# One convolution block goes from GpSimd to ScalarE and VectorE, and one input projection goes between two transposes

## The reference, cut to what matters

```python
zxbcdt = x @ in_proj_w.T
z = zxbcdt[..., :D_INNER]
xBC = zxbcdt[..., D_INNER:D_INNER + CONV_DIM]       # 384 channels
xp = jnp.pad(xBC, ((0, 0), (D_CONV - 1, 0), (0, 0)))
conv = conv_b
for k in range(D_CONV):                             # 4 taps
    conv = conv + xp[:, k:k + L, :] * conv_w[:, k]
xBC = jax.nn.silu(conv)
dt = jax.nn.softplus(zxbcdt[..., D_INNER + CONV_DIM:] + dt_bias)
```

## Time and profile before

| | |
|---|---|
| median of 3 runs | 872.43 us (872.13, 872.43, 874.5) |
| the profiled execution's own time | 876.48 us |
| its span | 874.8 us, granted clock 0.981 |
| PE busy | 796.5 us (91%) |
| VectorE busy | 605.7 us (69%) |
| ScalarE busy | 496.4 us (57%) |
| GpSimd busy | 365.4 us (42%) |
| GpSimd L1655, the sums of the convolution | 48 x 1302 ns = 62.5 us |
| GpSimd L1652, the products | 48 x 757 ns = 36.3 us |

### The profile page before, as it was taken

One profiled execution on the slowest core, in us unless ns is written; L12 is line 12 of the kernel. 1 busy time (PEld: TensorE's weight loads), 2 busy tenths in 40 slices (PEclk: granted clock), 3 DMA queues, 4 the chain that ended last, 5 costly groups with the idle time before them and its releaser, 6 DMA issues. The chain is left out here.

```text
span 874.8 us, 18230 instructions
## 1 busy us (share of the span) xinstructions
PE 796.5 (91%) x5472; PEld 492.2 (56%) x5472; DVE 605.7 (69%) x1443; ACT 496.4 (57%) x952; POOL 365.4 (42%) x656
## 2 busy tenths in 40 slices
PE   2789999999999999999899999999999998999897
PEld 1554564755647556565647555475555656475555
DVE  2576469784787757786687847877587866878534
ACT  2325774467743675547744678436854577446652
POOL 5633627054541627227280454516272272804500
PEclk9897999999999998999999999999999999999999
DMA  4000000000000100000000000000000000000000
GB/s 163 1 3 18 14 1 1 9 16 25 0 1 6 33 5 0 7 12 25 0 0 7 13 24 0 1 7 26 11 0 7 12 26 0 0 7 13 24 1 13
DMA packets 15145, 11.73 MB, mean 13 GB/s; under 512 B 1040, under 2 KB 13968, under 8 KB 14992
## 3 DMA queue, kind: packets, MB, share of 16 engines
q1 hardware_dynamic: 15120, 11.43, 4.3%
HBM read 7.76 MB, written 2.10 MB: 11 GB/s over the span
## 5 line engine op out<-in xcount | busy, mean ns | idle before, releaser
L1097 ACT ACTIVATE sb_pr<-S 128x768 f32<-128x768 f32 (+1 forms) x192 | 165.8, 890 | 130.8 <-PE S L444 130.8
L1194 DVE TENSOR_REDUCE sb_mx<-S 128x2 f32<-128x256 f32 (+3 forms) x256 | 197.7, 816 | 41.7 <-PE S L444 41.1
L1715 POOL TENSOR_SCALAR_AFFINE_SELECT sb_pr<-sb_pr 128x256 f32<-128x256 f32 (+1 forms) x192 | 98.9, 517 | 292.7 <-ACT sb_pr L1097 289.4
L444 PE MATMUL R<-sb_pr,sb_va 128*32 128x512 f32 (+3 forms) x1024 | 89.7, 445 | 0.0
L444 PE MATMUL S<-sb_kT,sb_qT 32*128 32x256 f32 (+3 forms) x512 | 56.8, 386 | 19.7 <-DVE sb_mx L1194 15.8
L444 PE MATMUL R<-sb_W,sb_pr 128*128 128x96 f32 (+1 forms) x512 | 69.5, 276 | 0.0
L444 PE MATMUL R<-sb_xfT,sb_W 128*128 128x512 f32 x144 | 69.2, 602 | 0.0
L444 PEld LDWEIGHTS S<-sb_kT,sb_qT 32*128 32x128 f32 x512 | 27.8, 184 | 73.0 <-DVE sb_mx L1194 65.2
L444 PEld LDWEIGHTS R<-sb_W,sb_pr 128*128 128x128 f32 x512 | 63.5, 192 | 3.8 <-issue 3.5
L1655 POOL TENSOR_TENSOR sb_cv<-sb_cv,sb_cm 128x512 f32<-128x512 f32 x48 | 62.5, 1302 | 4.0
L444 PE MATMUL S<-sb_qT,sb_kT 32*128 32x256 f32 (+3 forms) x512 | 56.8, 387 | 5.6 <-ACT sb_pr L1097 4.8
(11 more groups left out here) (216 smaller groups left out, 1711.2 us busy)
## 6 DMA issues: line engine op xcount, KB each, us to landing
sb_xin<-x SPq DMA_DIRECT2D x9, 256.0 KB, 2.7
sb_W<-weights SPq DMA_DIRECT2D x1, 2290.0 KB, 9.9
sb_qT<-sb_mT SPq DMA_DIRECT2D x128, 4.0 KB
sb_xres<-x SPq DMA_DIRECT2D x8, 256.0 KB, 2.8
out<-sb_xres SPq DMA_DIRECT2D x7, 256.0 KB, 2.3
sb_cT<-sb_xact SPq DMA_DIRECT2D x8, 128.0 KB, 2.3
sb_W<-weights SPq DMA_DIRECT2D x1, 514.0 KB, 4.6
sb_cst<-consts SPq DMA_DIRECT2D x1, 328.0 KB, 3.0
```

What stands on the lines that cost most here:

```text
L444: return pe.matmul(o, lhsT, rhs, start=start, stop=stop, skip_group_check=True)
L1097: act.activation(pr[:, e % 4, :, 0:n], S[pair_of_exp(e)][:, :, 0:n], ACT.Exp).then_inc(p_sb, 1)
L1194: o = dve.tensor_reduce(mx[:, n // P - 1, g, heads[0]:heads[1] + 1], found[:, :, at_col:at_col + n], AX.X, ALU.max, negate=True)
L1715: pool.affine_select(out=keep, in_=keep, compare_op=ALU.is_ge, fill=0.0, base=0, pattern=pattern, channel_multiplier=-1)\
```

## The change

It does three things. GpSimd keeps block 2 of the convolution alone (seven instructions less). Block 1 goes to ScalarE, which now makes the beginnings of blocks 0 and 1 ahead of the `qT` copies, and to VectorE, whose table now has six taps. On PE `project_x(r, 2)` moves from ahead of `project_z(r, 0)` to behind the transposes of `x1n`.

```diff
-TAP_AT = {2: (0, 2), 4: (0, 1), 6: (0, 0)}
+TAP_AT = {0: (0, 2), 2: (0, 1), 4: (0, 0), 6: (1, 2), 8: (1, 1), 10: (1, 0)}
...
                 if head:
                     project_x(r, 1)
-                    project_x(r, 2)
                     project_z(r, 0)
                     project_z(r, 1)
...
                 if head:
+                    project_x(r, 2)
                     project_z(r, 2)
...
                     evac_z(r, 3)
 
+                    for n in range(2):
+                        tap = V_CONVW + TAPS * n + TAPS - 1
+                        act.wait_ge(xc_sb, at(xc_sb, r, n + 1))
+                        act.wait_ge(conv_sb, at(conv_sb, r, 0))
+                        act.activation(cv[:, n], xc[:, n, TAPS - 1:TAPS - 1 + L], ACT.Identity,
+                                       bias=vec[:, V_CONVB + n:V_CONVB + n + 1],
+                                       scale=vec[:, tap:tap + 1]).then_inc(conv_act, 1)
                     act.wait_ge(e_ps, at(e_ps, r, 0))
...
-                    act.wait_ge(xc_sb, at(xc_sb, r, 1))
-                    act.wait_ge(conv_sb, at(conv_sb, r, 0))
-                    act.activation(cv[:, 0], xc[:, 0, TAPS - 1:TAPS - 1 + L], ACT.Identity,
-                                   bias=vec[:, V_CONVB:V_CONVB + 1],
-                                   scale=vec[:, V_CONVW + TAPS - 1:V_CONVW + TAPS]).then_inc(conv_act, 1)
...
-                    act.wait_ge(conv_dve, at(conv_dve, r, TAPS - 1))
-                    act.wait_ge(conv_pool, at(conv_pool, r, 2 * (2 * TAPS - 1)))
+                    act.wait_ge(conv_dve, at(conv_dve, r, 2 * (TAPS - 1)))
+                    act.wait_ge(conv_pool, at(conv_pool, r, 2 * TAPS - 1))
...
                 if k == TAPS - 2:
-                    dve.wait_ge(conv_act, at(conv_act, r, 1))
+                    dve.wait_ge(conv_act, at(conv_act, r, n + 1))
                 else:
-                    dve.wait_ge(conv_dve, at(conv_dve, r, 2 - k))
+                    dve.wait_ge(conv_dve, at(conv_dve, r, (TAPS - 1) * n + 2 - k))
...
-                    for n in (1, 2):
-                        base = at(conv_pool, r, (n - 1) * (2 * TAPS - 1))
+                    n = 2
```

More of the change, by code:

```diff
@@ L301, in build @@
         act_up = signal("act_up", 17)
-        conv_act = signal("conv_act", 1)
+        conv_act = signal("conv_act", 2)
         conv_sb = signal("conv_sb", 1)
@@ L331, in build @@
         kT_sb = signal("kT_sb", G)
-        conv_dve = signal("conv_dve", TAPS - 1)
+        conv_dve = signal("conv_dve", 2 * (TAPS - 1))
         mx_sb = signal("mx_sb", G * UNITS)
@@ L354, in build @@
         qw_sb = signal("qw_sb", 1)
-        conv_pool = signal("conv_pool", 2 * (2 * TAPS - 1))
+        conv_pool = signal("conv_pool", 2 * TAPS - 1)
         spa_sb = signal("spa_sb", 3)
@@ L1642, in stage_b @@
                     pool.sem_inc(pool_passed, 1)
-                    for n in (1, 2):
-                        base = at(conv_pool, r, (n - 1) * (2 * TAPS - 1))
[L1645 to L1655, removed]
+                    n = 2
+                    ts(cv[:, n], xc[:, n, 3:3 + L], vec[:, V_CONVW + 4 * n + 3:V_CONVW + 4 * n + 4],
+                       vec[:, V_CONVB + n:V_CONVB + n + 1], ALU.mult, ALU.add).then_inc(conv_pool, 1)
+                    for i, k in enumerate((2, 1, 0)):
+                        tap = V_CONVW + 4 * n + k
+                        if i:
+                            pool.wait_ge(conv_pool, at(conv_pool, r, 2 * i + 1))
+                            pool.sem_inc(pool_passed, 1)
+                        ts(cm[:], xc[:, n, k:k + L], vec[:, tap:tap + 1], 0.0, ALU.mult,
+                           ALU.add).then_inc(conv_pool, 1)
+                        pool.wait_ge(conv_pool, at(conv_pool, r, 2 * i + 2))
+                        tt(cv[:, n], cv[:, n], cm[:], ALU.add).then_inc(conv_pool, 1)
                     time_steps(r)
```

## The result

The changed kernel takes 866.6 us in the median of 20 runs (one, at 1860.09 us, lies far outside and is left out of every comparison; the other 19 lie at 862.86 to 874.31, with a median of 866.52) against 874.77 us for the kernel before (20 runs, 872.05 to 878.32): a ratio of 0.9912, 95% interval 0.9896 to 0.9929. Forecast were 869.5 us and a range of 865.5 to 876.0. The profiled execution took 864.34 us, its span is 862.6 us and its granted clock 0.993, against 876.48, 874.8 and 0.981.

A forecast was written before the change was run, and what follows sets the result against it. PE was taken as busy nearly all the time, slowed by clock falls and waits for VectorE. The profiled 876.48 us less 5.9 (clock) less 1.1 (seven rounds) gave 869.5 us, range 865.5 to 876.0, own range 868.0 to 871.0.

The forecast's parts named there:

- The clock: PE's tokqk transposes: with idle time moved away from just ahead, all three loop falls go, saving 5.9 us.
- The prologue: Rival: the clock also holds in the prologue's 32 transposes, 2.9 us less, 866.6 us; chance 0.08.
- ScalarE's delay: Two beginnings ahead of the first qT copy make PE wait about 0.5 us a round within the transposes.
- The rival that it is hidden: ScalarE's copies overlap, so PE never waits for qT: 4.6 us less in all, 866.0 us; chance 0.12.
- The lead of a round: Net gain of a loop round from VectorE's work: 0.15 us, 1.1 us over seven rounds.
- PE's group of g = 1: PE's wait of 0.88 us at its second score group goes; after the 0.5 us delay, PE is about 0.35 early.
- the tap behind m = 8: VectorE's added 0.66 us tap in 0.45 us of idle time: 0.2 too much, lead falls from 0.35 to 0.15.
- Behind m = 10: VectorE's added 0.66 us tap against 0.72 us back from the step freed of rs: lead stays 0.15 to 0.2.
- The meeting with `rs`: Rival: GpSimd's rs holds up VectorE's gate steps, 4.9 us more over seven rounds; 875.5 or 877.3 us; chance 0.20.
- The step behind m = 0: VectorE's added tap beside GpSimd's block may take 1.16 us, yet fits its idle time to within 0.1.
- The frame: Terms count from the profiled 876.48 us; the runs' median, 872.43, is 4.05 lower; without falls both meet near 870.6.

The follow-up runs named there:

- e1: Kernel before with only project_x(r, 2) moved behind the x1n transposes, convolution as before: ratio 0.9953 to the kernel before.
- e2: Changed kernel with project_x(r, 2) put back ahead of project_z(r, 0), so the convolution change alone: ratio 0.9958 to the kernel before.
- e8: Kernel before with four unread matmuls in PE's idle time ahead of the xf transposes, in the loop: ratio 0.9931 to the kernel before.
- e4: Changed kernel with four unread matmuls where the projection left, ahead of the x1n transposes, in the loop: ratio 0.9884 to the kernel before.
- e6: Changed kernel with the alterations of e3 and e4, plus six unread matmuls in the prologue: ratio 0.9811 to the kernel before.
- e7: e6 with block 1's last tap behind m = 12 instead of m = 10: ratio 0.9808 to the kernel before.
- e5: Changed kernel with GpSimd still doing its seven block 1 instructions, into an unread spare tile: ratio 0.9994 to the kernel before.
- e3: Changed kernel with ScalarE's two beginnings behind the fourth qT copy instead of ahead of the copies: ratio 0.9851 to the kernel before.

## Why the prediction was right, and what it mis-sized

- *The size and the luck in it.* The forecast of 869.5 is right to 0.3%, but not by its sum. From profile to profile it had 7.0 us (5.9 clock, 1.1 rounds) and the two profiles differ by 12.1; the range of its own, 868.0 to 871.0, missed 866.6. Two errors hid each other: the sum was too small by 2.1 us in the rounds and 4.1 in prologue and start, and too bold in that every fall would go, which the median run does not show.
- *The clock.* Right in its mechanism, which e1 against e2 and e8 show: where PE idles counts, and not only how much. Too bold in its size: that all falls go. One was left in this execution, for 4.9 us instead of 5.9, and six of the 19 runs, at 871.7 to 874.3 us with a mean granted clock of 0.978 to 0.980, must have several and the slow prologue, as e2's profile has; of the rest, 0.988 to 0.996, all but one lie under 867. The 0.93 us of idle time that only moved is what is left: filled (e4, e6, e7), the times near 872 us are gone. Why one round falls and the next, with the same times on PE ahead of it, does not, stays open. The three falls of the old profile cost 1.65 + 2.95 + 1.65 = 6.25 us by the lengths of their rounds, 0.35 more than the 5.9 of the sum.
- *The prologue.* I gave its clock 0.08 as a rival; it came true in this profile, and in those of e1 and e5, for 2.9 us. In e3 and e4 it did not, with the same stream on PE. The three profiles without the moved projection (before, e2, e8) all have slow transposes there. So the move may help, but does not decide; what does stays open. Filled, they took 3.7 us in both profiles (e6, e7).
- *ScalarE's delay.* 0.5 us a round forecast, 0.55 measured, all of it paid in an undisturbed round (e3). The rival that it is hidden is refuted there; it is true of the rounds in which the clock falls.
- *VectorE and GpSimd.* The lead of a round was 0.15 us in my sum and is 0.46. At PE's group of g = 1 I had 0.35 and it was 0.41 (442.58 - 416.81 = 25.77 against 26.18). The term that was mis-sized is the lead behind that group, in three steps. I took PE's 0.35 for VectorE's lead at the reduction of m = 8; but that reduction waits for nothing (454.08, 443.55) and follows VectorE's own work, which was 0.52 ahead at m = 6, so it came 0.49 ahead. With the tap behind m = 8 I let the lead fall by 0.2, and it fell by 0.1, to 0.38. Behind m = 10, where freed and added time were to cancel, it rose by 0.1. Seven rounds of 0.3 are 2.2 us. Had the sum gone by 0.46, it would have been 876.48 - 5.9 - 3.2 = 867.4.
- *The meeting with `rs`.* `rs` starts 27.05 us behind the `qk` product, as counted (453.9 in the old round). It misses. The step behind m = 0 did meet the product on GpSimd, and the tap still ended in time: the reduction behind it started at 433.82, 17.01 us behind the `qk` product, 0.55 later than before, which is ScalarE's delay.
- *The frame.* The three runs shown had a median of 872.43; twenty have 874.77. The forecast of 869.5 is 0.3% below the first and 0.6% below the second; measured is 0.9%.

## What to carry to other kernels

When an elementwise job goes from GpSimd to VectorE, count first what the GpSimd instruction did to VectorE's two-input instructions beside it: here the job cost three taps of 0.66 us, the first of them in idle time, and gave 1.06 us back ahead of a reduction for which PE waited (e5). An instruction put on an engine "which is idle there" is free only if the next thing on that engine is not awaited: two ACTIVATEs ahead of a PSUM copy cost 0.55 us in each undisturbed round, behind it nothing (e3). And where TensorE waits in a stretch of transposes and tiny matmuls, look at the granted clock of each round: unread matmuls in the idle time took 0.7% off the kernel before (e8), where the whole change took 0.9%.

## What was not expected of the hardware

- The same program ran at 862.9 to 874.3 us, and the time follows the mean granted clock (0.996 to 0.978); with PE's idle time filled the spread was 1.1 us (e6). A single run of such a kernel can be off by more than one per cent.
- A TENSOR_SCALAR of VectorE on 16 elements took 0.51 us at 432.75, where a free one takes 0.16: GpSimd was at a product until 433.22. So VectorE's one-input instructions between SBUF tiles can wait too.
